# Moving three pieces of DVE's hand-written order in a fused attention and FP4-FFN kernel

## The reference

```
x = x + 0.5 * ffn(layernorm(x))
x = x + attention(layernorm(x))        # 16 heads of 64, its own layernorm with gamma and beta inside
x = x + 0.5 * ffn(layernorm(x))

attention(x): q, k, v = x @ w_q, x @ w_k, x @ w_v
              o = softmax(q k^T / 8) v
              y = o @ w_proj + b_proj + x;  layernorm(y) * gamma + beta
ffn(x):       h = silu(fp4(x) @ fp4(w_gate)^T) * (fp4(x) @ fp4(w_up)^T)     # 352 wide
              fp4(h) @ fp4(w_down)^T
```

## Time and profile before

| what | value |
|---|---|
| runs | 2251.21, 2252.6, 2254.46 us (median 2252.6) |
| profiled execution, its own time | 2249.3 us |
| its span, first to last instruction | 2247.5 us |
| mean granted clock of TensorE | 0.982 |
| busy | PE 94%, DVE 71%, POOL 64%, ACT and weight loads 52% |

### The profile page before, as it was taken

The page is one execution under the profiler, slowest core; times in us unless marked ns, Lnnn a source line. Parts: engine busy times, 40 slices in busy tenths (PEclk is TensorE's granted clock), DMA queues, the critical chain, the costliest instruction groups (busy, mean ns, idle before and its releaser), DMA issues.

```text
span 2247.5 us, 39655 instructions
## 1 busy us (share of the span) xinstructions
PE 2103.3 (94%) x15049; PEld 1173.3 (52%) x15049; DVE 1605.0 (71%) x2627; ACT 1158.0 (52%) x1767; POOL 1427.2 (64%) x1289
## 2 busy tenths in 40 slices
PE   3999999999999999999999999999999999999984
PEld 2455555555555555555555555555555555555543
DVE  6675778777687777868777676877768777676643
ACT  2455555545555454555555455554554545455432
POOL 3365666757576675857657576675757667585652
PEclk8899999999999999999999999999999999999996
DMA  1000000000000000000000000000000000000000
GB/s 60 1 7 2 7 2 2 12 2 7 7 7 7 2 11 2 7 7 6 8 2 12 2 7 7 2 12 2 7 7 6 7 2 11 2 3 7 2 7 10
DMA packets 167498, 15.91 MB, mean 7 GB/s; under 512 B 148304, under 2 KB 166928, under 8 KB 167312
## 3 DMA queue, kind: packets, MB, share of 16 engines
q1 hardware_dynamic: 167312, 13.39, 5.1%
HBM read 7.03 MB, written 4.19 MB: 5 GB/s over the span
## 4 chain that ended last, share of the span: by engine, by line
PE 70%; DVE 17%; issue 4%; ACT 3%; SPq 2%; POOL 2%; DMA 1%; POOLq 0%; DVEq 0%
PE pS L957 18%; PE pO L985 14%; PE pX L1009 5%; PE pM L1095 4%; DVE nmax L810 4%; PE pX L969 4%; PE pO L941 4%; PE pM L941 3%; PE pM L997 3%; PE FpF L332 2%; PE LpF L332 2%; SPq L575 2%; PE FpF L295 2%; DVE ON L899 2%; PE LpF L308 2%
## 5 line engine op out<-in xcount | busy, mean ns | idle before, releaser
L683 POOL TENSOR_TENSOR ES<-ES,E 128x512 f32<-128x512 f32 x512 | 666.5, 1323 | 305.7 <-ACT E L760 303.1
L810 DVE TENSOR_REDUCE nmax<-pX 128x2 fp32r<-128x1024 f32 x512 | 623.3, 1217 | 240.0 <-PE pX L969 234.5
L760 ACT ACTIVATE E<-pS 128x1024 f32<-128x1024 f32 x512 | 523.8, 1023 | 518.9 <-PE pS L957 516.7
L985 PE MATMUL pO<-E,VA 128*64 128x512 f32 x2048 | 524.3, 611 | 5.9 <-DVE KL L911 5.8
L677 POOL TENSOR_TENSOR ES<-E 128x512 f32<-128x512 f32 x256 | 323.3, 1283 | 257.1 <-ACT E L760 257.1
L969 PE MATMUL pX<-KH,QH 64*128 64x512 f32 x1024 | 247.9, 424 | 21.7 <-DVE nmax L810 15.1
L957 PE MATMUL pS<-QH,KH 64*128 64x512 f32 x1024 | 253.9, 492 | 10.0 <-ACT E L760 10.0
L969 PEld LDWEIGHTS pX<-KH,QH 64*128 64x128 f32 x1024 | 187.7, 306 | 61.3 <-DVE nmax L810 27.4
L957 PEld LDWEIGHTS pS<-QH,KH 64*128 64x128 f32 x1024 | 95.9, 183 | 225.9 <-issue 220.1
L985 PEld LDWEIGHTS pO<-E,VA 128*64 128x64 f32 x2048 | 116.2, 135 | 172.3 <-issue 172.3
L957 PE MATMUL pS<-SH,onesr 64*128 64x512 f32 x1024 | 203.7, 393 | 0.0
(11 more groups left out here) (190 smaller groups left out, 3723.7 us busy)
## 6 DMA issues: line engine op xcount, KB each, us to landing
RROW<-RC SPq DMA_DIRECT2D x512, 2.0 KB, 2.0
xin<-in_L_attn_x SPq DMA_DIRECT2D x16, 256.0 KB, 2.9
SH<-nmax SPq DMA_DIRECT2D x256, 2.0 KB, 2.0
LC<-LROW SPq DMA_DIRECT2D x256, 2.0 KB, 2.1
out<-X SPq DMA_DIRECT2D x16, 256.0 KB, 2.5
E<-in_L_attn_w_q SPq DMA_DIRECT2D x1, 512.0 KB, 4.2
E<-in_L_attn_w_k SPq DMA_DIRECT2D x1, 512.0 KB, 5.3
wv<-in_L_attn_w_v SPq DMA_DIRECT2D x1, 512.0 KB, 7.1
```

Of the source, the lines that this page charges most:

```text
L683: ins = g.tensor_tensor(ES[i % 3][:, hd, :], ES[i % 3][:, hd, :], E[s][:, hd, :], ALU.add)
L760: a.activation(E[s][:, :, :], pS[:, :, :], ACT.Exp).then_inc(s_exp, 1)
L810: v.tensor_reduce(nmax[px % 2][:, :, t:t + 1], pX[:, :, :], AX.X, ALU.max, negate=True).then_inc(s_max, 1)
L985: ins = pe_.matmul(pO[half(hd), :], VA[of][:, kt, j * 128 + 64 * hd:j * 128 + 64 * hd + 64], E[kt][:, hd, :], start=kt == 0, stop=kt == KT ...
```

## The change

Two moves in DVE's body; no instruction is added or removed and no wait is changed. In quarter 3, ON goes behind silu, h and the maxima. In quarter 1, the FFN pieces (`first_ffn`, `last_ffn`) go in front of the addition to Yacc.

```
                         if s == 0 and p % 2 == 1 and there(i - 2, NP):
                             dve.wait_ge(s_lc, 64 * (i // 2))
                             v.reciprocal(REC[:, :, :], LC[:, :, :]).then_inc(s_rec, 1)
-                        if s == 3 and there(i - 3, NP):
-                            dve.wait_ge(s_rb, i - 2)
-                            wait(dve, s_proj, (i - 3) // 2)
-                            v.tensor_tensor(ON[(p - 3) % 2][:, :], OT[(i - 3) % 3][:, :], pM[:, :], ALU.mult).then_inc(s_norm, 1)
                         first_ffn_psum(b, t)
                         last_ffn_psum(b, t)
                         if s < 2:
                             maxima(i + 1, p + 1, s + 2)
                         else:
                             maxima(i + 2, p, s - 2)
+                        if s == 3 and there(i - 3, NP):
+                            dve.wait_ge(s_rb, i - 2)
+                            wait(dve, s_proj, (i - 3) // 2)
+                            v.tensor_tensor(ON[(p - 3) % 2][:, :], OT[(i - 3) % 3][:, :], pM[:, :], ALU.mult).then_inc(s_norm, 1)
...
+                        first_ffn(b, t)
+                        last_ffn(b, t)
                         if s == 1 and p % 2 == 1 and there(i - 4, NP):
                             bo, yp = (b, bpar) if p >= 4 else (b - 1, 1 - bpar)
                             dve.wait_ge(s_proj, (i - 3) // 2)
                             dve.wait_ge(s_y0, bo + 1)
                             wait(dve, s_yacc, (i - 5) // 2)
                             v.tensor_tensor(Yacc[yp][:, :], pX[:, 0, :], Yacc[yp][:, :], ALU.add).then_inc(s_yacc, 1)
-                        first_ffn(b, t)
-                        last_ffn(b, t)
```

More of the change, by code:

```diff
@@ L895, in body @@
                             v.reciprocal(REC[:, :, :], LC[:, :, :]).then_inc(s_rec, 1)
[L896 to L899, removed]
                         first_ffn_psum(b, t)
```

## The result

Four runs of the changed kernel gave 2294.42 to 2298.2 us, median 2297.15; the four of the kernel before, 2250.54 to 2254.46, median 2251.9. The ratio is 1.0198, 95% interval 1.018 to 1.0215: 45 us slower, where 24 were forecast. The profiled execution spans 2294.6 us, against 2247.5, and its mean granted clock is 0.970, against 0.982.

What follows compares the result with a forecast made beforehand. The prediction took nearly full TensorE (94% busy) as the bound. Waits of 1.64 us a full batch summed to 23.9, taking the profiled 2249.3 us to 2273.2; with 3.3 for the median, 2276.5 us, range 2254 to 2292.

Steps and rivals of the forecast that it cites:

- What bounds the kernel: TensorE, busy 94% of the span; DVE's order matters only where PE stands still for DVE.
- PE's three stops behind ON: In slots 7, 16 and 31 PE waits for DVE pieces behind ON, losing .70, .99 and .53 us.
- slot 3: Value round L1095 must wait for the later ON: a loss of 1.10 us in each of 15 batches.
- Part 1: ON behind silu, h and maxima: most of three PE stops comes back, slot 3 loses 1.10 us.
- Slots 7, 16 and 31: PE stops where DVE makes ON first; gains of .70, .99 and .53 us in 13 batches.
- Part 2: Roundings in front of the addition to Yacc: slot 5's move costs .34 us, slot 13's 2.42.
- Slot 6: pX starts later because slot 5's roundings delay Yacc: a loss of .34 us in 14 batches.
- Slot 13: Roundings take turns with POOL's sums, delaying Yacc and pX of slot 14: a loss of 2.42 us in 13 batches.
- the reading by today's lengths: In slot 13, roundings taking only the 1.43 and .89 us seen before the change: a loss of 1.67.
- The sum: All losses less gains: 1.64 us a full batch, 23.9 in all, giving a median of 2276.5 us.
- the third rival: PE's stand in slot 14 brings half clock 13 times, costing up to 22 us more: 2298.5 us, chance .08.

Runs made afterwards that it cites:

- the fourth run: The kernel before with ON moved behind silu, h and the maxima, except in slot 3, and the FFN pieces left in place: 2223.46 us, ratio 0.9876.
- The short sum: The changed kernel with POOL's first sum of exponentials for pair 3 cut to 16 of 512 columns: 2257.31 us, ratio 1.0019.
- the second: The kernel before with only the FFN pieces moved in front of the addition to Yacc, ON unmoved: 2288.45 us, ratio 1.016.
- the last run: The fourth run with the FFN pieces in front of the addition to Yacc in slot 13 alone: 2260.17 us, ratio 1.0035.
- the first run: The kernel before with only ON moved behind silu, h and the maxima, FFN pieces unmoved: 2243.5 us, ratio 0.996.

## Why the forecast was wrong, point by point

- *What bounds the kernel* was right: PE's three stops behind ON were real, and taking away most of them, with nothing lost in slot 3, is worth 28 us (the fourth run, which leaves .12 in slot 7 and .39 in slot 16).
- *Part 1.* Slot 3: 1.10 forecast, 1.17 in the trace, and 1.23 a batch between two runs. Slots 7, 16 and 31: all three stops gone in the changed kernel, as forecast.
- *Part 2.* Slot 6: .34 forecast, .35 seen up to the start of pX and .47 up to that of pO. Slot 13: 2.42 forecast, 2.45 seen, by the turns with POOL's sum that were read from the earlier trace rows. The short sum shows that these turns are the cause. By the Trainium skill's rule (SBUF — State Buffer, Who interferes with whom) it is 2.42 as well, and the trace agrees with 2.45; the reading by today's lengths, 1.67 (1.61 by its own figures, 1.06 and .55 for the longer L220), does not hold.
- *The sum* of the waits was right: 1.64 a batch forecast, 1.7 in the run that fills the gap, and that run's 2274.18 us stands 2.3 under the forecast of 2276.5.
- *The step that failed* is the weighing of the third rival, "The clock falls". It had a chance of .08 and lay outside the range, and the sum put the clock at nothing. The runs showed 13 falls of the clock behind slot 14's gap, worth 23 of the 45 us. The rival was weighed too low by the argument that no row of the full-clock stretch shows a gap of this length. That argument speaks for neither side. The one row that bore on it, the fall at 2182 us in the tail, spoke for the rival: it begins some .3 before the end of a gap of 2.06 us, the longest that the kernel before has between 76 us and there, and shorter than the one forecast. The prediction says only "a stretch with gaps" of it:

```profile
2182.33 1.44 PE L308 MATMUL LpF<-wguT,LxqT 128*64 128x352 f32 x4 [2.06 <-DVE Lh L374]
```

- The forecast had made a new gap more than twice as long as any between 76 and 2175 us (1.02) and left the clock as it was.
- The rival names the place. That its price comes so close, 2298.5 against 2297.15 measured, is in part luck. Half of 3.4 us for each fall, 1.7, is a little more than the 1.55 to 1.6 seen for one of 3.41, that three of 13 falls lasted twice as long and cost 2.9 was not foreseen, and with the same gap two other orders of the pieces had falls in 11 and in 5 of 13 batches.
- The Trainium skill (TensorE: Matmul & The Clock Gate, Why this matters for your kernels) warns of idle gaps between bursts of matmuls, but of longer ones than slot 14's. The runs differ: behind gaps of 2.28 us the clock fell in 13, 11 and 5 of 13 batches; behind those of 1.0 us it never fell.

What stays open is why one gap of 2.28 us is followed by a fall and the next, equally long and in the same place of the program, is not. The programs of the second and the last run differ from the changed kernel only in where DVE's pieces stand, and in the length of a batch. That it depends on when the gap comes is argued from this, and was not tried. Nor does a longer gap always bring a fall: in the tail of the first run one of 3.14 us ends at 2175.37, and the clock stays at 1.00 for more than 4 us behind it:

```profile
2175.37 0.81 PE L308 MATMUL LpF<-wguT,LxqT 128*64 128x352 f32 x4 [3.14 <-DVE Lh L374]
...
2176.00:2180.20 4.20, 1.93 (x34) 1.67 (x30) 2.19 (x3) 0.79 (x1) 0.88 (x1) 1.00 0.11 8
```

## What to carry to other kernels

On an engine that works in order, a piece may go behind another only where nobody waits for it sooner: the same move won in three slots and lost in a fourth, and leaving that one slot alone turned 0.4% faster into 1.2%. When a forecast opens an idle gap on TensorE that is longer than any gap the trace shows at full clock, take the fall of the clock into the range, at its price (here 1.6 us for a fall of 3.41 us), and not into a small chance: in these runs it followed such a gap in all, most or some of the batches, and the length alone did not tell which. A gap that can't be closed can be filled: 1.8 us of products that nobody reads, in a bank that is free, made the changed kernel 23 us faster, though not faster than the kernel before.

## What the runs showed of the hardware that had not been expected

The granted clock fell at idle stretches of TensorE of 2.28 us, between .5 us before their end and 1.7 us after it, for 3.41 or 6.83 us, and at none of up to 1.30 us in the steady part of any run (100 to 2150 us); a fall of 3.41 us cost 1.55 to 1.6 us, one of 6.83 us some 2.9. In three programs with the same gap it fell in 13, 11 and 5 of 13 batches; a gap of 1.72 to 1.74 us in batch 1 of the same three brought it down in one. In the tail of the first run a gap of 3.14 us passed without one.
